# Late fills on GpSimd, a re-dealt first stack, filler products, and a last finish that scales behind its products

## The reference, cut to what matters

```python
h   = layernorm(x)
q, k, v = split(h @ w_qkv)                 # 16 heads x 8
q, k = rope(q), rope(k)
attn = softmax(where(causal, q @ k.T * 8**-0.5, -inf))
x   = x + (attn @ v) @ w_out
h   = layernorm(x)
base = h @ base_W.T + base_b
shared = (h @ shared_A.T) @ shared_B.T     # rank 16
gate = softmax(h @ router_W.T + router_b)  # 6 experts
w    = top-2 of gate, divided by their sum + 1e-6
routed = sum_e w_e * ((h @ routed_A[e].T) @ routed_B[e].T)
out = x + base + shared + routed
```

## Time and profile before

| | |
|---|---|
| median of 3 runs | 319.71 us (319.04 to 320.12) |
| the profiled execution's own time | 319.8 us |
| its span in the profile | 318.1 us |
| TensorE busy | 285.8 us (90%) |
| ScalarE busy | 269.6 us (85%), of it 253.9 us in 280 exps (L588) |
| VectorE busy | 146.3 us (46%) |
| GpSimd busy | 57.5 us (18%) |
| mean granted TensorE clock | 0.973 |

### The profile page before, as it was taken

One profiled execution on the slowest core, in us unless ns is written; L12 is line 12 of the kernel. 1 busy time (PEld: TensorE's weight loads), 2 busy tenths in 40 slices (PEclk: granted clock), 3 DMA queues, 4 the chain that ended last, 5 costly groups with the idle time before them and its releaser, 6 DMA issues.

```text
span 318.1 us, 7501 instructions
## 1 busy us (share of the span) xinstructions
PE 285.8 (90%) x3006; PEld 103.8 (33%) x3008; DVE 146.3 (46%) x425; ACT 269.6 (85%) x300; POOL 57.5 (18%) x129
## 2 busy tenths in 40 slices
PE   7948883989899989899999998999999999999896
PEld 2613241222223422123313313443533333433353
DVE  6775596468875376956241003651000514101064
ACT  8567584779999798999999999999999999999700
POOL 0485141031330300403003020101001010110100
PEclk9966998799999999999999999999999999999999
DMA  6333137000550000160000100000100000000000
GB/s 173 112 93 92 26 103 190 10 1 2 152 148 0 23 15 1 35 165 2 0 3 0 36 2 2 0 3 2 35 2 3 2 2 0 2 19 2 3 0 16
DMA packets 15400, 11.75 MB, mean 37 GB/s; under 512 B 2033, under 2 KB 14178, under 8 KB 15362
## 3 DMA queue, kind: packets, MB, share of 16 engines
q1 hardware_dynamic: 14866, 10.90, 12.6%
q10 hardware_dynamic: 432, 0.20, 0.2%
q0 software_dynamic: 64, 0.13, 0.1%
HBM read 3.88 MB, written 1.05 MB: 16 GB/s over the span
## 4 chain that ended last, share of the span: by engine, by line
PE 37%; ACT 22%; DVE 21%; issue 15%; DMA 2%; SPq 1%; DVEq 1%; POOL 0%; ACTq 0%; POOLq 0%
ACT pbuf L588 22%; PE po L962 17%; PE ps L940 9%; PE pm L978 3%; DVE rest L665 3%; DMA xs<-x_dram 2%; PE ps L1082 2%; DVE rot L672 2%; DVE absmax L696 1%; PE pm L1021 1%; PE pm L1015 1%; DVE oq L647 1%; DVE rot L659 1%; DVE rest L682 1%; PE pm L972 1%
## 5 line engine op out<-in xcount | busy, mean ns | idle before, releaser
L588 ACT ACTIVATE pbuf<-ps 128x1024 f32<-128x1024 f32 (+1 forms) x280 | 253.9, 1068 | 24.6 <-PE ps L940 24.2
L962 PE MATMUL po<-pbuf,va 128*9 128x256 f32 (+3 forms) x1792 | 146.7, 433 | 9.3 <-DVE oq L647 7.0
L940 PE MATMUL ps<-qst,kst 64*128 64x256 bf16 (+3 forms) x896 | 97.7, 303 | 8.1 <-ACT pbuf L588 3.4
L537 POOL TENSOR_SCALAR_AFFINE_SELECT pbuf<-pbuf 128x256 f32<-128x256 f32 (+1 forms) x104 | 48.9, 492 | 231.6 <-ACT pbuf L588 230.4
L940 PEld LDWEIGHTS ps<-qst,kst 64*128 64x128 bf16 x896 | 30.3, 95 | 104.0 <-ACT pbuf L588 77.2
L962 PEld LDWEIGHTS po<-pbuf,va 128*9 128x9 f32 x1792 | 35.6, 90 | 66.7 <-issue 42.8
L647 DVE STREAM_TRANSPOSE oq<-po 128x256 f32<-128x256 f32 (+1 forms) x24 | 12.9, 536 | 84.7 <-PE po L962 84.4
L665 DVE TENSOR_TENSOR rest<-pm,sinT 32x512 f32<-32x512 f32 x16 | 11.0, 687 | 0.3
L978 PE MATMUL pm<-xnT,wqkv 128*128 128x512 f32 x16 | 9.0, 644 | 1.9 <-DVEq L812 1.3
L1082 PE MATMUL ps<-kst 128*128 128x512 bf16 x44 | 10.5, 379 | 0.2 <-issue 0.2
L806 DVE COPY lowT<-pm 113x512 f32<-113x512 f32 (+1 forms) x5 | 2.9, 585 | 16.6 <-PE pm L1029 16.6
(11 more groups left out here) (115 smaller groups left out, 184.6 us busy)
## 6 DMA issues: line engine op xcount, KB each, us to landing
qst<-parts SPq DMA_DIRECT2D x18, 128.0 KB, 2.4
kst<-parts SPq DMA_DIRECT2D x18, 128.0 KB, 2.5
xs<-x_dram SPq DMA_DIRECT2D x4, 256.0 KB, 4.1
cosT<-rope_c_dram SPq DMA_DIRECT2D x4, 256.0 KB, 4.4
sinT<-rope_s_dram SPq DMA_DIRECT2D x4, 256.0 KB, 5.6
out_dram<-xs SPq DMA_DIRECT2D x3, 256.0 KB, 2.3
kst<-parts SPq DMA_DIRECT2D x11, 64.0 KB, 2.1
qst<-parts SPq DMA_DIRECT2D x8, 64.0 KB, 2.0
```

Of the source, the lines that this page charges most:

```text
L537: ins = nc.gpsimd.affine_select(out=edge, in_=edge, compare_op=ALU.is_ge, fill=0.0, base=0, pattern=[[0, edge.shape[1]], [1, P]], channel_ ...
L588: nc.scalar.activation(probs[:, :, 0:width], ps[:, u % NS, :, 0:width], ACT.Exp, scale=SCALE).then_inc(exp_ready, 1)
L940: ins = nc.tensor.matmul(ps[:, u % NS, e, place:place + n], side(kst, e)[:, g * 2 + pair, key:key + P], side(qst, e)[:, g * 2 + pair, q:q ...
L962: ins = nc.tensor.matmul(po[32 * j:32 * j + DH + 1, q0:q0 + n], va[:, kt, g * GH + j, :], pbuf[:, u % NPB, at:at + n], start=blk["first"] ...
```

## The change

1. **Fills.** ScalarE fills `kst` of chunks 0, 1, 2 and `qst` of chunk 0, all before unit 0; the fill of `qst` chunk 2 behind unit 7 is gone. GpSimd fills `qst` of chunk 1 at its start, and the rest (`LATE_FILLS`: `qst` of chunk 2, `kst` and `qst` of chunk 3) as twelve memsets of one tile each (8x64 float32 words a partition), one before the mask of each of units 24 to 35. VectorE's two memsets are gone.
2. **Start.** The tables of rope for chunk 0 are loaded in two halves, with the rows of chunk 1 between them. All six key slots go over SyncE's queue, Q0, Q3, Q4 over ScalarE's, Q1, Q2 over GpSimd's. VectorE sets the first flag before the second part's query rope and not behind it; TensorE no longer waits for both value copies before the bound's sum. GpSimd's inverse root has 12 steps for 14. Filler products: 6 and 4 bfloat16 ones around the bound's sum for 3 and 1 float32 ones, 3 new ones before the first scores and 2 new ones behind each of units 0 to 3.
3. **Places.** B and K1 of part 1 move from place 5 to 3; in the pieces behind, some twenty jobs move by one or two places.
4. **Last group.** In the last group of the last piece the two diagonal units come first, and the last block of two units is split into two of one.
5. **Last finish** (`end_of_chunk`). The rows are only centred before X; the inverse root runs behind them, and logits and the final sum are scaled afterwards (`scalar_tensor_tensor`). ScalarE copies X's product and the shared rank; the ranks are ordered on the logits beside ScalarE's exp; direct semaphores take the place of `job_fed`. Each of the two tiles is stored by itself. Filler products before X, R, U, F: 7, 2, 14, 2 for 16, 3, 16, 3.

```diff
-FIRST_BY_SP = (("K", 0), ("K", 1), ("K", 2), ("Q", 0), ("K", 3), ("K", 4), ("Q", 5))
-FIRST_BY_ACT = (("Q", 1), ("Q", 3), ("Q", 4))
-FIRST_BY_POOL = (("Q", 2), ("K", 5))
+FIRST_BY_SP = (("K", 0), ("K", 1), ("K", 2), ("K", 3), ("K", 4), ("K", 5), ("Q", 5))
+FIRST_BY_ACT = (("Q", 0), ("Q", 3), ("Q", 4))
+FIRST_BY_POOL = (("Q", 1), ("Q", 2))
...
+    if last:
+        wide = wide[-2:] + wide[:-2]
...
+            if end:
+                work[-1:] = [[unit] for unit in work[-1]]
...
-WARM = {"O": 8, "X": 16, "R": 3, "U": 16, "F": 3}
+LATE_FILLS = ([("Q", 0.0, 2 * TC + t) for t in range(TC)]
+              + [("K", ONE_ONE, 3 * TC + t) for t in range(TC)] + [("Q", 0.0, 3 * TC + t) for t in range(TC)])
+LATE_FILL_UNITS = range(FIRST_UNIT[2], FIRST_UNIT[2] + len(LATE_FILLS))
+WARM_O, WARM_X, WARM_R, WARM_U, WARM_F = 8, 7, 2, 14, 2
-WARM_BOUND = 3
-WARM_FLAG = 1
+WARM_BOUND = 6
+WARM_FLAG = 4
+WARM_KEYS = 3
+WARM_UNITS = (2, 2, 2, 2)
...
-    (1, 1, 2, 5, 5, 6),
+    (1, 1, 2, 3, 3, 6),
...
# sync
-            load_chunk(0)
-            load_chunk(1)
+            load_rows(0)
+            sp.dma_start(idf[:, :], ident).then_inc(ident_in, 16)
+            sp.dma_start(wqkv[:, :, :], w_qkv).then_inc(qkv_in, 16)
+            load_rope(0, 0, HALF_CH)
+            load_rows(1)
+            load_rope(0, HALF_CH, CH)
+            load_rope(1)
...
# gpsimd
+            fill(qst, 0.0, TC, TC)
...
             for u, unit in enumerate(UNITS):
+                if u in LATE_FILL_UNITS:
+                    stacked, value, tile = LATE_FILLS[LATE_FILL_UNITS.index(u)]
+                    fill(kst if stacked == "K" else qst, value, tile, 1)
                 if not unit["diagonal"]:
                     continue
...
# scalar
-            fill_queries(1)
+            fill_keys(2)
...
-            fill_keys(2)
...
-                if u + 1 == FIRST_UNIT[1]:
-                    fill_queries(2)
...
# vector
             bound(0).then_inc(bound_ready, 1)
-            rope_second("Q")
             dve.wait_ge(bound_full, 1)
             set_flag(0, pm[:, :])
+            rope_second("Q")
             rope_second("K")
...
-                    if NEW_PREP[FIRST_UNIT.index(u)] == 2:
-                        last = slice((NC - 1) * CH, NC * CH)
-                        nc.vector.memset(kst[:, :, last].bitcast(F32), ONE_ONE).then_inc(filled_last, 1)
-                        nc.vector.memset(qst[:, :, last].bitcast(F32), 0.0).then_inc(filled_last, 1)
...
+            def end_of_chunk():
...
+                dve.wait_ge(end_summed, 1)
+                then(nc.vector.tensor_tensor(xs[:, tiles, :], by_tile, xs[:, tiles, :], ALU.add))
+                spread(END, 0, nt)
+                for t in range(nt):
+                    nc.vector.tensor_scalar(ln[:, t, :], xs[:, END + t, :], mv[:, 0, t, 0:1], None,
+                                            ALU.subtract).then_inc(end_rows, 1)
+                inverse_sqrt(nc.vector, then, 0, nt)
+                then(nc.vector.tensor_tensor(low_rank[:, 0:nt, RD], var[:, 0, 0:nt], scale[:, 0:nt], ALU.mult))
...
+                dve.wait_ge(end_full, 1)
+                for t in range(nt):
+                    nc.vector.scalar_tensor_tensor(xs[:, END + t, :], last[:, t, :], scale[:, t:t + 1], xs[:, END + t, :],
+                                                   ALU.mult, ALU.add).then_inc(y_ready, 1)
...
# tensor
-            keep_warm(WARM_BOUND, wqkv[:, 0, :], xnT[:, 0, :])
+            hot = kst[:, 0, CH:CH + P], kst[:, 0, CH:2 * CH]
+            pe.wait_ge(filled, FILLS_BY_ACT[1])
+            keep_warm(WARM_BOUND, *hot)
             pe.wait_ge(const_in, 16 * 4)
-            pe.wait_ge(v_ready, 2)
+            pe.wait_ge(v_ready, 1)
...
                 scores(u)
+                if u < len(WARM_UNITS):
+                    keep_warm(WARM_UNITS[u], *hot, pm[:, :])
```

217 lines of the change are left out of this document (152 added, 65 removed), and 6 rows, old and new, of the table PLACES.

## The result

Median of 4 runs after the change: **307.89 us** (307.79 to 308.76), beside 319.38 us (318.76 to 320.12) for 4 runs before on the same chip: a ratio of 0.964, 95% interval 0.961 to 0.967. The forecast was 310.3 us, its range 308.2 to 313.3. Chance in the clock decided on which side of the bound the median fell.

A forecast was written before the change was run, and what follows sets the result against it. ScalarE bounds the last 50 us of exps, so gains come where it stands still: tail 2.7, hole 5.1, start 1.4 and places 0.3 sum to 9.5 us, taking 319.8 to 310.3 us; range 308.2 to 313.3.

The forecast's parts named there:

- The tail: Chain behind the last exp, to the span's end: shortened in three places, lengthened in one; 2.7 us won, bounds 2.0 and 3.3.
- Rows before root: Tail, end of moments to logits: centring first, root beside the other branch, 2.6 us for 4.25; 1.65 us won.
- Routing: Tail, logits to scaled ranks: ranks ordered on logits with the exp beside them, and cheaper handovers; 0.45 us won.
- Last store: Span's end: two sums and two stores for one each, the second issued about 0.35 us later; 0.3 us lost.
- The hole: Unit 24: without VectorE's memsets the transposition comes 3.83 us earlier and TensorE stays fast; 5.1 us won, bounds 3.8 and 5.6.
- The start: Stretch up to unit 24: earlier second rows and flag, clock kept by new fillers; 1.4 us won, bounds 0.2 and 2.6.
- The places: Jobs moved by two places give VectorE time and take it from nobody; 0.3 us won, bounds -0.8 and 1.0.
- The port rule: Objection at the hole: GpSimd memsets lock ports shared with VectorE, blocking its copies or scalar operations; sum 1 us smaller.
- 1 (the front half swallows its gains): VectorE's chain sets units 3 to 24 and up to unit 42, so less is won there; 313.0 us, chance 0.22.
- 2 (more than summed): Load gives 1.6 us, clock holds from the first scores, ScalarE left only exps; 11.5 us won, 308.3 us, chance 0.13.
- 3 (the tail turns cold): With 25 fillers for 38 the clock falls to 1.2 GHz before the last products; 312.3 us, chance 0.07.
- 4 (fills too slow): GpSimd's fills delay unit 32's masks from 1.4 us each; 328 us at 3.4 us a fill, chance 0.05.

The follow-up runs named there:

- warm_through: Changed kernel with longer filler rows: 10 for 6 before the bound's sum, 7 for 4 behind it, 11 for 2 behind unit 3; median 307.84 us, ratio 0.963.
- bound_at_5: Changed kernel with B and K1 of part 1 back at place 5; median 308.63 us, ratio to before 0.966.
- slow_fills: Changed kernel with three more 512-word GpSimd memsets into a spare tile behind each late fill; median 323.83 us, ratio to before 1.015.
- memsets_back: Changed kernel with the chunk 3 fills taken from GpSimd and VectorE's two memsets back at unit 24; median 314.30 us, ratio to before 0.982.
- memsets_back_warm: As memsets_back, plus 18 filler products on TensorE while it waits for VectorE's transposition; median 312.45 us, ratio to before 0.976.
- root_first: Changed kernel with the inverse root ahead of the two centred rows again in the last finish; median 311.98 us, ratio to before 0.975.
- one_store: Changed kernel with the last two tiles stored by one DMA behind both sums; median 309.62 us, ratio to before 0.970.

## Why the prediction was right in kind and short in size

Point by point, by its own steps.

- **The tail: 3.25 us for 2.7.** *Last block*: 1.02 for 0.9, inside its bounds. *Rows before root*: 1.9 for 1.65; the two centred rows take 0.48 us for the 0.60 taken over from the scaled ones, and VectorE and the other branch meet with nothing left over. *Routing*: from logits to scaled ranks 3.32 for 3.69, so 0.37 for 0.45. *Last store*: a loss of 0.12 us (2.79 for 2.67) and not 0.3, all of it in the second sum; the second store's issue, taken as added to the end, wasn't.
- **The hole: 5.8 us for 5.1.** The mechanism is as forecast. VectorE's stay was 4.1 us for 3.83: the idle time ahead of it fell as well (1.09 us for 1.36), which no run explains. The step that fell short is "16 products in 0.84 us for 1.89, 1.05 us more", counted once. Those sixteen gave 0.84 us (1.89 for 1.05), but TensorE's slow stretch went on through the scores and the next sixteen values to the second transposition, and VectorE's chain to T3 starts there: the clock was worth 1.84 us, not 1.05.
- **The start: 1.5 us for 1.4**, but the sum hides what was not known: the load gives 0.95 us as forecast (measured on warm_through), the rest hangs on the clock, which holds in some executions only. "With eight new fillers TensorE is busy nearly without a gap there" was wrong: it waits 2.25 us at unit 3, and with the bound at place 5 it would wait 2.13 (bound_at_5). That the clock held all the same in the profiled execution and in two of the three beside it was luck. In executions in which it falls the start gives 0.2 us, its lower bound.
- **The places: 1.4 us for 0.3**, the term most off and the step that failed. "Behind the hole ScalarE's waits are short" is not so as a whole (one of 1.89 us stands at 109.39), and where ScalarE is the bound their sum is what counts: 10.42 us in the trace of before. "Most stand behind products that don't move" holds, for 8.83 us are left; but some 1.35 us stood behind ones that do. I looked at one window of the last 50 us and took it for the whole stretch.
- **The price of a fill**: 0.52 to 0.60 us for 512 words, one every 0.47 us where they stand in a row, below the 0.65 taken from the mask of that size; 2048 words took 1.87 us at the start. Cover and end came out as argued (nine in 4.26 us, 4.31 us to spare).
- **The port rule** of the Trainium skill (SBUF — State Buffer, Who interferes with whom), weighed in part 2: a block of VectorE for a whole memset isn't seen. In slow_fills GpSimd clears memory nearly without a break from 49.3 us, and the longest that a single instruction of VectorE stretches is 0.45 us for 0.17, while four rows of normalisation take 1.53 us (1.27 before). VectorE's chain from the second transposition to T3 takes 6.83 us there, 6.65 after the change, 6.53 before it, and 6.34 and 6.36 in memsets_back and memsets_back_warm, where GpSimd's fills are over by then. So fills beside VectorE cost 0.1 to 0.3 us in the change and 0.5 without a break. By that rule the sum was to be 1 us smaller.

**The rivals.** 1 (the front half swallows its gains): no; VectorE's chain to T3 did move with the transposition. 2 (more than summed): its 308.3 us came nearest, but by luck: it had 2.6 us for the start, which gave 1.5, and too little for the places and the tail. 3 (the tail turns cold): no, with 25 fillers the granted clock is 1.00 from 291.3 to 303.2 us; in root_first it fell behind a wait of TensorE of 1.9 us. 4 (fills too slow): real, but at four times what a fill takes; at 2.21 us a fill the kernel is already slower than before by 1.5%, where the working put the crossing at 2.5.

The four errors, 0.1, 0.7, 1.1 and 0.6 us, all have one sign and make the 2.5 us between 9.5 and 12.0. The places and the hole's clock are over two thirds of it. The low end, 308.2, took the upper bounds of two parts only; with those of all four it would have been 319.8 - 3.3 - 5.6 - 2.6 - 1.0 = 307.3 us. The hole and the places lie above their own upper bounds (5.8 for 5.6, 1.4 for 1.0), the start and the tail within theirs. Part of the difference is the execution that was profiled before the change: 319.8 us at a clock of 0.973, where other runs of that kernel came out at 318.0 to 320.9 us and 0.973 to 0.979.

## What to carry to other kernels

Where one engine is the bound over a long stretch, add up all its waits in that stretch before costing a re-ordering: four of about 0.35 us were 1.4 us here. When a stall goes, count the slow clock behind it for every chain that passes through, and not only for the one that waited. Look at several executions before believing a gain that rests on the clock, and look at filler products at the slow clock as well: a row that fits at full clock can end behind the data at half of it, as fourteen did in root_first (4.16 us for 3.19). A shorter row there was not run.

## What the runs showed of the hardware

- The same program, with the same 2.25 us of idling at the same place, came out of it at 2.4 GHz in one execution (twelve products 0.72 us) and at 1.2 in another (1.25 us). That alone makes two groups of times (307.7 to 307.9 and 309.1 to 309.9 us), which look like noise of the measurement.
- A GpSimd memset of 128 partitions by 512 float32 words takes 0.52 to 0.60 us, and one ends every 0.47 us where they stand in a row; by 2048 words it takes 1.87 us, where VectorE's took 1.76. The two engines are about as fast at it.
- A second store of half the size, issued 0.4 us behind the first, ended 2.18 us behind its data, and one store of the whole 2.24 us behind them (one_store).
- A chain of 24 instructions of VectorE, from the second transposition to T3, stretched from 6.34 us to 6.83 while GpSimd cleared memory beside it nearly without a break.
